# Two mixture-of-experts stages of a perceiver kernel: one PSUM accumulator each, gates applied before the hidden activations are turned, biases written by matmuls

## The reference, cut to what matters

```
gup = einsum(x, gate_up_proj) + 2 * (x A_e) B_e          # per expert, 256 wide
gates, h = split(gup);  h = silu(gates) * h              # 128 wide
out = h down_proj + 2 * (h A'_e) B'_e                    # 256 wide
y = sum over the 2 chosen experts of weight_e * out_e
```

```
h = relu(flat @ w1_e + b1_e);  y_e = h @ w2_e + b2_e
gating = scores of the 4 best / their sum ;  shared experts have weight 1
out = flat + sum_e gating_e * y_e
```

## Time and profile before

| what | us |
|---|---|
| median of three runs | 1068.96 (1065.78 to 1069.72) |
| profiled execution | 1068.2 |
| its span | 1066.4 |
| stage 5, from the last add of stage 4 to its own last add | 403.0 to 423.4 |
| stage 11, from PE's first dummy matmul to DVE's last add | 1039.7 to 1063.9 |
| PE busy over the span | 1002.6 (94%) |
| DVE, ACT, POOL busy | 721.9, 365.7, 156.8 |

### The profile page before, as it was taken

How to read it: one execution, slowest core, us unless ns; L and a number is a source line. 1 busy time by engine, 2 the same in 40 slices (tenths; PEclk the granted TensorE clock), 3 DMA queues, 4 the chain that set the end, 5 groups by cost and what they waited for, 6 DMA issues and landing times.

```text
span 1066.4 us, 20794 instructions
## 1 busy us (share of the span) xinstructions
PE 1002.6 (94%) x7883; PEld 656.4 (62%) x7883; DVE 721.9 (68%) x1918; ACT 365.7 (34%) x662; POOL 156.8 (15%) x143
## 2 busy tenths in 40 slices
PE   6999999998799988898999999999999998988988
PEld 4776676665335544365777767677777776743554
DVE  3777767768779835677676767767676867753344
ACT  2332333234327731433333333333343332311204
POOL 0000000001000010233232323222222323000000
PEclk9999999999999999999999999999999999899999
DMA  7100101002229996850000000000000000233530
GB/s 283 41 22 24 36 20 40 20 5 95 99 77 186 185 329 238 301 206 2 1 1 2 1 0 0 0 0 0 0 0 0 0 2 1 80 139 109 209 146 4
DMA packets 69161, 77.33 MB, mean 73 GB/s; under 512 B 52592, under 2 KB 59504, under 8 KB 65648
## 3 DMA queue, kind: packets, MB, share of 16 engines
q1 hardware_dynamic: 68672, 75.93, 22.8%
q10 hardware_dynamic: 432, 0.64, 0.2%
HBM read 63.65 MB, written 0.07 MB: 60 GB/s over the span
## 4 chain that ended last, share of the span: by engine, by line
PE 73%; DVE 11%; issue 6%; ACT 3%; POOL 3%; DMA 3%; SPq 0%; DVEq 0%; POOLq 0%
PE ps L2202 15%; PE ps L2163 12%; PE ps L1487 8%; PE ps L2192 7%; PE ps L1477 4%; PE ps L1498 4%; PE ps L1521 2%; PE ps L1533 2%; POOL x_sum L2726 2%; ACT vals L2023 2%; DMA x_keys<-vals 2%; DVE S L2418 1%; PE ps L504 1%; PE ps L1881 1%; PE ps L2810 1%
## 5 line engine op out<-in xcount | busy, mean ns | idle before, releaser
L2202 PE MATMUL ps<-vals,S 128*128 128x257 f32 x784 | 188.2, 383 | 0.7 <-ACT S L2652 0.7
L2163 PE MATMUL ps<-keysT,row_biases_sb 128*128 128x512 f32 (+1 forms) x416 | 185.5, 571 | 0.4 <-DVE row_biases_sb L2382 0.3
L2726 POOL TENSOR_TENSOR x_sum<-x_max,consts 128x4 f32<-128x4 f32 (+1 forms) x104 | 133.7, 1285 | 322.8 <-DVE x_max L2406 322.8
L2418 DVE SCALAR_TENSOR_TENSOR S<-ps,x_sum,keysT 128x128 f32<-128x128 f32 x392 | 110.9, 345 | 71.4 <-PE ps L2202 63.0
L2202 PEld LDWEIGHTS ps<-vals,S 128*128 128x128 f32 x784 | 143.1, 192 | 18.9 <-issue 1.0
L2652 ACT ACTIVATE S<-S 128x512 f32<-128x512 f32 (+1 forms) x104 | 62.7, 606 | 219.2 <-DVE S L2453 218.7
L2192 PE MATMUL ps<-x_q,x_keys 128*128 128x128 f32 x784 | 113.2, 286 | 0.0
L2163 PEld LDWEIGHTS ps<-keysT,row_biases_sb 128*128 128x128 f32 x416 | 76.4, 191 | 56.5 <-issue 51.4
L2192 PEld LDWEIGHTS ps<-x_q,x_keys 128*128 128x128 f32 x784 | 95.6, 191 | 0.0
L1487 PE MATMUL ps<-ring,S 128*128 128x512 f32 x196 | 92.6, 594 | 0.5 <-DVE ps L1628 0.5
L2640 ACT COPY x_keys<-ps 128x512 f32<-128x512 f32 (+1 forms) x104 | 57.1, 549 | 64.3 <-PE ps L2192 34.2
(11 more groups left out here) (453 smaller groups left out, 1380.2 us busy)
## 6 DMA issues: line engine op xcount, KB each, us to landing
ring<-weights SPq DMA_DIRECT2D x24, 1024.0 KB, 5.9
keysT<-ctxT SPq DMA_DIRECT2D x2, 3136.0 KB, 14.8
vals<-ctxN SPq DMA_DIRECT2D x1, 6272.0 KB, 24.6
S<-ctxT SPq DMA_DIRECT2D x12, 512.0 KB, 4.0
keysT<-weights SPq DMA_DIRECT2D x6, 864.0 KB, 8.6
ring<-weights SPq DMA_DIRECT2D x6, 768.0 KB, 7.2
ring<-weights SPq DMA_DIRECT2D x2, 864.0 KB, 5.4
row_biases_sb<-row_biases SPq DMA_DIRECT2D x1, 1416.0 KB, 12.2
```

The source lines that it names most:

```text
L2163: ins = pe.matmul(ps[:, c % 3, 0:width(c)], x2_wk[:, k, :], ctxT[:, k, span(c)], start=k == 0, stop=k == KT - 1)
L2202: ins = pe.matmul(bank(6, D + 1), S[:, a:a + TILE], ctx_and_ones[:, SUB * c + s, :], start=c == 0 and s == 0, stop=c == NC - 1 and s == su ...
L2418: ins = dve.scalar_tensor_tensor(S[:, a:a + TILE], ps[:, 3 + c % 2, 128 * s:128 * s + 128], x2_inv[:, c % 2, s:s + 1], x2_tile_const, ALU. ...
L2726: pool.tensor_tensor(x2_inv[:, c % 2, 0:n], x2_var[:, c % 2, 0:n], C("neg_half").broadcast_to([128, n]), ALU.pow)\
```

## The change

In stage 5 every pair gets its own gate and up bank (2 to 5), so `up(n)` waits for nobody; the order on PE becomes up 0, up 1, up 2, turn 0, up 3, turn 1, down 0, turn 2, down 1, turn 3, down 2, down 3. The expert weight, with the 0.5 of the silu, is multiplied in by DVE's second hidden operation, from a table for both halves (`f1_pair_gates`). All `down(n)` and the low-rank product accumulate in bank 0, and `x` gets two adds at the end. The low-rank part is scaled as soon as its own last matmul is done.

In stage 11 PE first writes `b1` of all nine pairs into PSUM: `f3_select`, 128 rows by 128 columns for a pair, is a copy of identity columns that ACT makes during stage 10, so that one matmul puts expert 2m's bias into rows 0 to 63 and expert 2m + 1's into 64 to 127. Nine such matmuls stand ahead of the norm; the dummy ones fall from nine to three. The nine hidden products are accumulated onto them in nine half banks (0 to 4), the shared pair first. ACT applies relu to the shared pair, DVE relu and gate to the other eight in one operation each. The 1584 hidden columns then stand side by side and are turned in 13 tiles of 128 (the last has 48), four tiles to a PSUM bank, in four groups; ACT copies each group in one operation. `output(q)` multiplies each tile with all 128 rows and accumulates everything, `b2` last, in bank 6. Two adds to `x` end the stage. The weights come in four pieces for `w1` (the fourth late) and two late ones for `w2`.

```diff
+F3_UP = (("f3_up0", 0, 2), ("f3_up1", 2, 4), ("f3_up2", 4, 6), ("f3_up3", 6, F3_PAIRS))
+F3_DOWN = (("f3_down0", 0, 7), ("f3_down1", 7, F3_TILES))
+F3_LATE = ["f3_up3", "f3_down0", "f3_down1"]
+    + [(11, n, F3_UP_WIDTH * (b - a) + (F3_GATE if a == 0 else 0)) for n, a, b in F3_UP]
+    + [(11, n, 2 * D * (b - a)) for n, a, b in F3_DOWN]
...
-                     10: (4, 1), 11: (9, 3)}
+                     10: (4, 1), 11: (3, 5)}
...
 # f1_tensor
-                if n >= 2:
-                    pe.wait_ge(sem("f1_hidden"), since("f1_hidden", n - 1))
-                out = [ps[rows_of(i), 2 + n % 2, 0:256] for i in range(2)]
+                out = [ps[rows_of(i), 2 + n, 0:256] for i in range(2)]
...
+                if n == 3:
+                    ins.then_inc(sem("f1_lows_psum"), 1)
-                    ins = pe.matmul(ps[rows_of(i), 4 + n % 2, 0:D], f1_h[:, 2 * n + i, :], W(f"f1_experts{n}")[:, a:a + D],
-                                    start=True, stop=True, skip_group_check=True)
+                    ins = pe.matmul(ps[rows_of(i), 0, 0:D], f1_h[:, 2 * n + i, :], W(f"f1_experts{n}")[:, a:a + D],
+                                    start=n == 0, stop=n == 3 and i == 1, skip_group_check=True)
...
 # f1_vector
+            for i in range(2):
+                ins = dve.tensor_scalar(f1_pair_gates[rows_of(i), :], cut(f1_p, 4, 2)[:, :, i], f1_sum, 0.5, ALU.mult, ALU.mult)
...
+                link(dve, "dve", dve.scalar_tensor_tensor(act, act, 1.0, g, ALU.add, ALU.mult))
+                dve.scalar_tensor_tensor(act, act, f1_pair_gates[:, n:n + 1], u, ALU.mult, ALU.mult).then_inc(sem("f1_hidden"), 1)
+            dve.wait_ge(sem("f1_lows_psum"), since("f1_lows_psum", 1))
...
+            residual_vector(dve, 5, bank(0, D, T), (sem("f1_lora_psum"), since("f1_lora_psum", 1)))
+            link(dve, "dve", dve.tensor_tensor(x[:, :], x[:, :], ps[rows_of(1), 0, 0:D], ALU.add))
...
 # a3_scalar
+            act.copy(cut(f3_select, NE, T), spread(C("ident")[:, 0:NE], 2, T)).then_inc(sem("f3_selected"), 1)
...
 # f3_tensor
+            pe.wait_ge(sem("f3_selected"), since("f3_selected", 1))
+            for m, pair in enumerate(F3_ORDER):
+                pe.matmul(f3_bank(m), f3_select[:, 128 * pair:128 * pair + 128], b1, start=m % 2 == 0, stop=False, skip_group_check=True)
             norm_tensor(pe, 11)
...
+            for name, first, end in F3_UP:
+                weights_here(pe, name)
+                for m in range(first, end):
+                    for k in range(KT):
+                        for c in range(2):
+                            a = F3_UP_WIDTH * (m - first) + 2 * FF * k + FF * c
+                            ins = pe.matmul(f3_bank(m)[rows_of(c), :], xnT[:, k, 0, :], W(name)[:, a:a + FF], start=False, stop=k == KT - 1,
+                                            skip_group_check=True)
+                    ins.then_inc(sem("f3_hidden_psum"), 1)
+            def turn(q):
+                if q == 0:
+                    pe.wait_ge(sem("f3_first"), since("f3_first", 1))
+                pe.wait_ge(sem("f3_gated"), since("f3_gated", min(-(-512 * (q + 1) // FF), F3_PAIRS) - 1))
+                if q >= 2:
+                    pe.wait_ge(sem("f3_hT"), since("f3_hT", q - 1))
+                b = (5, 7)[q % 2]
+                for j in f3_tiles(q):
+                    n = f3_rows(j)
+                    ins = pe.transpose(ps[0:n, b, 128 * (j % 4):128 * (j % 4) + 128], f3_hidden[:, 128 * j:128 * j + n], C("ident"))
+                if q == F3_GROUPS - 1:
+                    pe.wait_ge(sem("f3_gates_ready"), 1)
+                    ins = pe.transpose(ps[0:NE, b, 448:512], f3_gates, C("ident")[0:T, 0:T])
+                ins.then_inc(sem("f3_hT_psum"), 1)
+            def output(q):
+                pe.wait_ge(sem("f3_hT"), since("f3_hT", q + 1))
+                for j in f3_tiles(q):
...
+                    for c in range(2):
+                        a = 2 * D * (j - first) + D * c
+                        pe.matmul(ps[rows_of(c), 6, 0:D], f3_hT[0:n, j, T * c:T * c + T], W(name)[0:n, a:a + D], start=j == 0,
+                                  stop=c == 1 and j == F3_TILES - 1, skip_group_check=True)
             turn(0)
+            for q in range(F3_GROUPS):
+                if q + 1 < F3_GROUPS:
+                    turn(q + 1)
+                output(q)
+            pe.matmul(bank(6, D, T), f3_gatesT, b2, start=False, stop=True, skip_group_check=True).then_inc(sem("f3_out_psum"), 1)
...
 # f3_vector, behind the router
+            for m in range(1, F3_PAIRS):
+                pair = F3_ORDER[m]
+                dve.wait_ge(sem("f3_hidden_psum"), since("f3_hidden_psum", f3_with(m)))
+                dve.tensor_scalar(f3_hidden[:, FF * m:FF * m + FF], f3_bank(m), 0.0, f3_pair_gates[:, pair:pair + 1], ALU.max, ALU.mult)\
+                   .then_inc(sem("f3_gated"), 1)
             link(dve, "dve", dve.tensor_tensor(x[:, :], x[:, :], xn[:, :], ALU.add))
...
+            residual_vector(dve, 11, bank(6, D, T), (sem("f3_out_psum"), since("f3_out_psum", 1)))
+            link(dve, "dve", dve.tensor_tensor(x[:, :], x[:, :], ps[rows_of(1), 6, 0:D], ALU.add))
```

More of the change, by code:

```diff
@@ L213, in pack_piece @@
     w2 = np.concatenate([a["L3_ffn_routed_w2"], a["L3_ffn_shared_w2"]], 0)
[L214 to L219, removed]
+    if name.startswith("f3_up"):
+        _, first, end = F3_UP[last]
+        up = [k_major(np.concatenate([w1[2 * F3_ORDER[m]], w1[2 * F3_ORDER[m] + 1]], 1)) for m in range(first, end)]
+        if first > 0:
+            return cat(*up)
+        b1, b2 = [rows(np.concatenate([a[f"L3_ffn_routed_{b}"], a[f"L3_ffn_shared_{b}"]], 0)) for b in ("b1", "b2")]
+        return cat(*up, tr("L3_ffn_centroids"), b2, b1)
+    _, first, end = F3_DOWN[last]
+    joined = np.zeros((128 * F3_TILES, 2, D), np.float32)
+    for m, pair in enumerate(F3_ORDER):
+        joined[FF * m:FF * m + FF] = w2[2 * pair:2 * pair + 2].transpose(1, 0, 2)
+    return k_major(joined.reshape(128 * F3_TILES, 2 * D)[128 * first:128 * end])
 ROW_BIASES = (("bv0", D), ("bo0", D), ("a0_qkv", 3 * D), ("a0_out", D), ("kv1", 2 * D), ("q1", D), ("out1", D),
@@ L474, in W @@
             if n in late:
-                a = pieces[n][2] * late.index(n)
+                a = sum(pieces[i][2] for i in late[:late.index(n)])
                 return keysT[:, :, :].rearrange("p k n -> p (k n)")[:, a:a + pieces[n][2]]
@@ L1302, in f3_tensor @@
             norm_tensor(pe, 11)
             normT_here(pe, 11)
[L1304 to L1305 removed]
             for k in range(KT):
[L1307 removed]
+                ins = pe.matmul(ps[0:T, 7, D:D + 16], xnT[:, k, 0, :], w[:, 16 * k:16 * k + 16], start=k == 0, stop=k == KT - 1)
             ins.then_inc(sem("f3_logits_psum"), 1)
[L1310 to L1319 removed]
@@ L1321, in turn @@
-            def turn(n):
-                pe.wait_ge(sem("f3_copied"), since("f3_copied", n + 1))
-                if n >= 2:
-                    pe.wait_ge(sem("f3_relu"), since("f3_relu", n - 1))
-                for i in range(2):
-                    ins = pe.transpose(ps[0:FH, 3 + n % 2, 128 * i:128 * i + 128], f3_hidden[n % 2][:, FH * i:FH * i + FH], C("ident"))
-                ins.then_inc(sem("f3_hT_psum"), 1)
-            def output(n):
-                pe.wait_ge(sem("f3_relu"), since("f3_relu", n + 1))
-                if n >= 3:
-                    pe.wait_ge(sem("f3_added"), since("f3_added", n - 2))
-                for i in range(2):
-                    for e in range(2):
-                        a = 4 * FF + D * (2 * e + i)
-                        ins = pe.matmul(f3_out(n)[T * e:T * e + T, :], f3_h[n % 2][:, i, e, :], W(f"f3_experts{n}")[0:FH, a:a + D],
-                                        start=i == 0, stop=i == 1, skip_group_check=True)
-                ins.then_inc(sem("f3_expert_psum"), 1)
@@ L1340, in f3_tensor @@
-            hidden(0)
-            hidden(1)
-            turn(0)
-            for n in range(NE // 2):
-                if n + 2 < NE // 2:
-                    hidden(n + 2)
-                if n + 1 < NE // 2:
-                    turn(n + 1)
-                output(n)
-                if n == 2:
-                    pe.wait_ge(sem("f3_gates_ready"), 1)
-                    pe.transpose(ps[0:NE, 6, D:D + T], f3_gates, C("ident")[0:T, 0:T]).then_inc(sem("f3_gatesT_psum"), 1)
-                if n == 3:
-                    pe.wait_ge(sem("f3_gatesT_ready"), since("f3_gatesT_ready", 1))
-                    pe.matmul(bank(6, D, T), f3_gatesT, w[0:NE, 32:288], start=True, stop=True).then_inc(sem("f3_bias_psum"), 1)
+            for name, first, end in F3_UP:
[7 more added lines that the diff above has]
+                    ins.then_inc(sem("f3_hidden_psum"), 1)
@@ L2939, in load @@
                     reload_ctxN(sp)
-                if late and name == "f3_experts1":
+                if late and name == "f3_up1":
                     sp.wait_ge(sem("x3_scores_psum"), since("x3_scores_psum", X3_PAIRS + 1))
```

176 lines of the change are left out of this document (65 added, 111 removed), and 4 rows, old and new, of the table shared.

## The result

The changed kernel's median over 12 runs is 1067.06 us (1062.17 to 1068.81), that of the kernel before over 12 runs 1069.26 us (1065.78 to 1074.94). The recorded ratio is 0.9964, with a 95% interval of 0.9948 to 0.9980: 3.8 us faster, in bounds of 2.1 and 5.6, and within the 0.5% that the prediction took for no change. It is not the ratio of the two medians; these lie 2.2 us apart (0.9979, inside the interval). The sum had forecast 0.9964 (1064.3 against 1068.2). As a time, 1067.06 lies in the whole range of 1061.5 to 1067.5, but 0.6 above the forecast's own of 1063.0 to 1066.5: the sum started from the profiled 1068.2, and the median of the kernel before is 1069.26.

What follows compares the result with a forecast made beforehand. The prediction took PE to bound stage 11, with 1.81 us of DVE tail, and stage 5. From 1068.2 us it subtracted 3.84 and 0.06 to reach 1064.3, own range 1063.0 to 1066.5, with rivals 1 to 3 1061.5 to 1067.5.

Steps and rivals of the forecast that it cites:

- The sum: Whole kernel: 1068.2 less 3.84 in stage 11 and 0.06 in stage 5 gives 1064.3 us.
- Term 1: Stage 11's start: bias matmuls (2.80 us) and three dummies (0.70) overrun the norm, moving the start back by 1.13 us.
- Rival 1: Stage 11's bias matmuls: each pass takes its stream and then its weight load, 2.07 us more, 1066.4; 12%.
- The gates: Stage 11 on DVE: router shifts, ending at 1049.03, then eight relu-and-gate operations at 0.385 us each.
- PE from there: Stage 11 after the gates: PE waits 0.15 and 0.5 us for DVE's gating and ends 3.0 us earlier, shift included.
- Term 3: End of stage 11: DVE's tail of four operations, 1.81 us, becomes two adds, 0.93; 0.88 us less.
- Stage 11 in all: All of stage 11: DVE ends at 1060.05 instead of 1063.89, 3.84 us less.
- term 4: Stage 5: earlier low-rank part, less a second add to x, gains 0.06 us, in bounds of 0 and 0.5.
- Rival 2: Stage 5: the half-clock stretch doesn't return, about 1.7 us, giving 1062.6, faster by 0.52%; 20%.
- Rival 3: Stage 11: norm and bias matmuls finish together, so term 1 is near 0.1, giving 1063.3; 8%.
- Rival 4: Stage 11: PE drops to the lower clock, 8.7 us of work doubles, up to 1073.0; 5%.
- Beside the path: Off the critical path: ACT's identity copy (1.24 us) falls into its idle time, and late loads land long before use.

Runs made afterwards that it cites:

- Kernel 1: Changed kernel without its nine bias matmuls, with nine dummy matmuls ahead of the norm as before: stage 11 took 19.33 us against 20.74.
- kernel 3: Changed kernel without the three dummy matmuls between the biases and the norm of stage 11: stage 11 took 20.10 us against 20.74.
- kernel 4: Kernel before with all stage 11 expert outputs accumulated in one bank, two adds at the end, gates left out: stage 11 took 23.38 us against 24.24.
- kernels 8 and 9: Kernel before (8) and changed kernel (9), each with four more dummy matmuls in stage 5: stage 5 took 19.20 and 17.91 us.
- kernels 11 and 12: 11: changed kernel, five bias matmuls moved into stage 10, stage 5 ring slots handed back one turn later, ratio 0.9956; 12: that plus four stage 5 dummies, 0.9946.
- kernels 5 and 10: 5: changed kernel, stage 5's low-rank part scaled late again, stage 5 18.38 us; 10: changed kernel, five of nine bias matmuls moved into stage 10, ratio 0.9954.
- kernel 6: Kernel before with the change of stage 5 alone: ratio 0.9993 (0.9970 to 1.0016), stage 5 17.90 us.

## Why the prediction was right, point by point

**The sum:** that 0.9964 was forecast and measured is in part luck. By the profiles stage 11 gave 0.34 less than forecast and stage 5 0.24 more, errors inside stage 11 cancelled too (see below), and the interval reaches 1.7 us to either side.

**Term 1, the start moves back by 1.13 us:** right in kind, 1.40 in size (3.77 against 2.37). The eighteen passes took 2.92, 0.162 each instead of 0.156, and PE began 0.27 us after DVE's add, not 0.11. Kernel 1 shows that it is on the path in full, kernel 3 that the three dummies are 0.65 of it.

**Rival 1, exposed weight loads:** refuted. The eighteen loads ran beside the passes, as the timeline of after shows:

```profile
1043.96 2.68 PEld L1309 LDWEIGHTS ps<-ring,S 128*128 128x128 f32 x18 [0.73 <-issue]
```

The two shapes agree: 0.453 for 512 columns and 0.162 for 176 are 0.87 ns a column and 0.01 us besides. With a load of 0.115 in each, the first would leave 0.66 ns a column, and the second would be 0.23. The prediction's argument for this was wrong in a step: 512 columns at one a cycle of 2.4 GHz are 0.213 us, not 0.427. By the rows a float32 pass takes about two such cycles a column (0.88 ns), and a bf16 dummy of 512 columns, 2.10 / 9 = 0.233 us, about one. The rule of the Trainium skill (TensorE: Matmul & The Clock Gate, What overlaps and what doesn't), by which these loads would not overlap, does not hold for these matmuls.

**The gates:** right. The router took 4.53 us (1048.83 to 1053.36) where 4.51 stood. The gate operation was mis-sized: 0.385 was taken, five took 1.65, 0.33 each. That is 0.27 less up to the second turn, and it hides what the start lost: that turn comes 11.36 us after the add that ends stage 10, where 11.35 was forecast.

**PE from there:** the two holes came where they were named, ended by DVE's gating. Groups of instructions of after, stage 11:

```profile
L1350 PE MATMUL ps<-keysT,S 128*64 128x256 f32 x48 | 5.8, 385 | 0.0
...
L1382 DVE TENSOR_SCALAR S<-ps,S 128x176 f32<-128x176 f32 x8 | 2.6, 393 | 0.0
...
L1335 PE MATMUL ps<-consts,S 128*128 128x128 f32 x12 | 1.9, 284 | 0.5 <-DVE S L1382 0.5
```

They are 0.25 and 0.21 us, together 0.5, where 0.15 and 0.5 were forecast. From 1055.08 to the end of the last matmul it is 8.42 instead of 8.11: the turn of group 1 took 0.66 (0.59 was taken), the last turn with the gates 0.37 (0.25), the last outputs 2.46 (2.35).

**Term 3, the tail, 0.88:** 0.86 in kernel 4, and 0.96 us from PE's end to DVE's in after instead of 1.81.

**Stage 11 in all:** 3.50 instead of 3.84. Term 1's 0.27 and the gates' cancel, so the 0.34 is the 0.31 behind the second turn and 0.03 in the tail.

**Stage 5, term 4, 0.06 within 0 and 0.5:** 0.30 in the pair of profiles. Of this 0.13 lies in the end of the stage, where 0.06 was forecast (the low-rank part came 0.49 earlier for 0.51, the second add took back 0.36 for 0.45). The other 0.17 lies ahead of it, and no kernel isolates it. The step that failed is the sentence before the term: "PE is the bound and its work is the same". That holds in an execution with the half-clock stretch, which was the only one I had. At full clock the router's wait at turn 0 is the bound, and the change is worth 1.29 there (kernels 8 and 9), by the chains above through `up(2)`'s move ahead of that wait; no kernel changes the order alone. A gain in stage 5 above 1 us was one of the prediction's own signs of being wrong. By the profiles the change is thus worth 3.5 us in stage 11 and something between 0.3 and 1.3 in stage 5, and the ratio's 2.1 to 5.6 us allow either; how often each case occurs in the timed runs is not known, and their scatter would hide it.

**Rival 2, the stretch that doesn't return:** it was rightly kept apart from the code. It stayed out of stage 5 in 5 of the 14 profiles, three of them with the added dummies, and in either kernel's version of the stage (in that of before only with them). But it was priced as a gain of the change of 1.7; it is a property of the execution, and what it frees is 0.3 before (19.52 to 19.20) and 1.3 after (19.22 to 17.91).

**Rival 3, covered biases:** not so here, but possible; kernels 11 and 12 reach it with other code.

**Rival 4, half clock in stage 11:** not in the profile of after, nor when the last three dummies went (kernel 3). It is not excluded: the profiles of kernels 5 and 10 have such a stretch across the start of that stage, and stage 11 is 21.32 in kernel 5, 0.58 more than in after. It fell there in stage 10, ahead of the changed code, and 14 profiles do not tell whether the change makes it likelier.

**Beside the path:** ACT's copy took 1.15 us (1.24 was taken) and ended 5 us ahead of the bias matmuls; the late loads were in long before use.

## What to carry to other kernels

Matmuls that fill a wait are free only up to the wait's end; count them against it in time, not in number, and spread them over the waits of the stage before. Take an independent matmul out from behind a wait on PE's queue even if the one profile at hand shows PE busy there: at the other clock level the wait is the bound. And when two spans differ by less than the stretches at half clock are worth, compare stage by stage. Here most stages repeat within 0.1 us and stages 2 and 9 come in two groups, while stages 0 and 6 vary by 3 to 4 us each and the runs scatter by 6 to 9 us.

## What the runs showed of the hardware that was not expected

The stretches at the 1.2 GHz level come at the same few places of the program, in one execution and not in the next: stage 2 (1.6 us), stage 9 (1.63 us), stage 5 and two places of stage 6. Where PE is not the bound they cost little (0.3 us in the stage 5 of before, 1.3 in that of after), so their price depends on the kernel. PE had been busy 4.25 of the 5.90 us ahead of after's stretch in stage 5; this is the view of the busy times by stretch, and then the same place in kernel 6, where the clock did not fall:

```profile
406.00:411.90 5.90, 4.25 (x28) 2.64 (x30) 2.55 (x10) 0.47 (x2) 0.54 (x1) 1.00 0.64 185
```

```profile
404.68:410.58 5.90, 4.25 (x28) 2.65 (x30) 2.55 (x10) 0.47 (x2) 0.54 (x1) 1.00 0.65 191
```

The two rows are alike, so what PE did there does not alone decide whether the clock falls. The Trainium skill (TensorE: Matmul & The Clock Gate, The HAM clock gate) says that in one and the same kernel the number of matmuls that run at the lower clock varies from run to run. The profiles agree: the stretch of stage 5 comes in some and not in others, and where it comes it begins 3.8 to 4.7 us after the norm's power. All three profiles with the four added dummies (kernels 8, 9 and 12; PE is busy 5.05 of these 5.90 us in kernel 9) were free of it in stage 5, against 2 of the 11 without them. That suggests that a busier PE keeps it away there; three profiles don't show it.
